# The low part of x: from a GpSimd subtraction to an accumulating DMA and ScalarE, with x and the projection weights split in the opposite sign

## The reference

```
R, K, V = x @ Wr.T, x @ Wk.T, x @ Wv.T
lif:  v = v + (x_t - v) * 0.5;  s = (v >= 1);  v = v * (1 - s)
h = h * 0.9 + k * v;  y = r * h                     # per step, k, v, r are spikes
x1 = layernorm(x + y @ Wo.T) * g1 + b1
s1 = lif_scan(x1 @ W1.T + b1);  ffn = lif_scan(s1 @ W2.T + b2)
a  = layernorm(x1 + ffn) * g2 + b2
x3 = layernorm(x + a)                               # the kernel: mean and variance only
g  = top-2 of softmax(x3 @ Wg + bg), renormalised
out = layernorm(x3 + sum over the 2 chosen experts of g_e * (x3 @ We[e] + be[e]))
```

## Time and profile before

| | us |
|---|---|
| three runs | 1040.43, 1044.15, 1044.51 (median 1044.15) |
| the profiled execution | 1044.85, its span 1043.0 |
| busy: TensorE / VectorE | 965.0 / 965.0 |
| busy: ScalarE / GpSimd | 540.0 / 580.4 |

### The profile page before, as it was taken

The page is one execution under the profiler, slowest core; times in us unless marked ns, Lnnn a source line. Parts: engine busy times, 40 slices in busy tenths (PEclk is TensorE's granted clock), DMA queues, the critical chain, the costliest instruction groups (busy, mean ns, idle before and its releaser), DMA issues.

```text
span 1043.0 us, 22651 instructions
## 1 busy us (share of the span) xinstructions
PE 965.0 (93%) x7552; PEld 935.1 (90%) x7552; DVE 965.0 (93%) x3860; ACT 540.0 (52%) x1256; POOL 580.4 (56%) x720
## 2 busy tenths in 40 slices
PE   5567788999999999999999999999999999899884
PEld 5567777999999999999999999999999999899884
DVE  5888897999999999999999999999999999998765
ACT  4333323456655555555665555555566555455351
POOL 1000122666666676776666666677666666665451
PEclk8878878999999999999999999999999999999998
DMA  4310111344555444544455545454445554446662
GB/s 158 99 52 31 31 41 41 70 91 87 110 102 112 102 104 97 105 101 91 88 108 102 112 102 107 98 102 102 90 87 108 102 112 92 98 95 115 132 126 65
DMA packets 53109, 98.30 MB, mean 94 GB/s; under 512 B 5888, under 2 KB 5888, under 8 KB 52992
## 3 DMA queue, kind: packets, MB, share of 16 engines
q0 software_dynamic: 31392, 57.16, 32.3%
q1 hardware_dynamic: 16992, 31.30, 9.3%
q10 hardware_dynamic: 4608, 8.39, 2.1%
HBM read 31.29 MB, written 8.39 MB: 38 GB/s over the span
## 4 chain that ended last, share of the span: by engine, by line
PE 79%; DVE 14%; ACT 3%; issue 2%; POOL 1%; DMA 0%; POOLq 0%; DVEq 0%; ACTq 0%
PE ps_e L349 30%; PE ps_proj L349 12%; PE ps_proj L404 11%; PE ps_proj L419 9%; PE ps_attn L385 6%; PE ps_proj L425 5%; DVE U L723 3%; DVE V L730 3%; PE ps_zx L393 2%; DVE h L774 1%; PE ps_attn L393 1%; DVE stats L804 1%; POOL s L1161 1%; DVE x_lo L852 1%; ACT x L577 1%
## 5 line engine op out<-in xcount | busy, mean ns | idle before, releaser
L349 PE MATMUL ps_e<-we_hi,x_hi 128*128 128x256 f32 (+1 forms) x1024 | 296.3, 289 | 5.1 <-ACT odd_sum L596 3.2
L349 PE MATMUL ps_e<-we_lo,x_hi 128*128 128x256 f32 (+1 forms) x1024 | 287.6, 281 | 0.0
L349 PE MATMUL ps_e<-we_hi,x_lo 128*128 128x256 f32 (+1 forms) x1024 | 287.5, 281 | 0.0
L730 DVE SCALAR_TENSOR_TENSOR V<-U 128x256 f32<-128x256 f32 (+5 forms) x656 | 249.2, 390 | 0.7
L723 DVE SCALAR_TENSOR_TENSOR U<-V,U 128x256 f32<-128x256 f32 (+5 forms) x656 | 238.0, 373 | 0.9
L559 ACT ACTIVATE U<-ps_proj,cst 128x256 f32<-128x256 f32 x320 | 135.5, 480 | 175.9 <-PE ps_proj L404 98.2
L1147 POOL TENSOR_SCALAR veps<-mv 128x2 f32<-128x2 f32 x128 | 53.9, 421 | 284.1 <-DVE mv L810 284.1
L349 PEld LDWEIGHTS ps_e<-we_hi,x_hi 128*128 128x128 f32 x1024 | 193.5, 189 | 10.6 <-ACT odd_sum L596 8.4
L1161 POOL TENSOR_SCALAR s<-U 128x256 fp32r<-128x256 f32 x208 | 192.5, 951 | 7.7 <-DVE V L730 7.7
L349 PEld LDWEIGHTS ps_e<-we_hi,x_lo 128*128 128x128 f32 x1024 | 193.9, 189 | 0.1
L349 PEld LDWEIGHTS ps_e<-we_lo,x_hi 128*128 128x128 f32 x1024 | 193.1, 189 | 0.0
(11 more groups left out here) (87 smaller groups left out, 2187.7 us busy)
## 6 DMA issues: line engine op xcount, KB each, us to landing
acc<-term POOLq DMA_DIRECT2D x93, 256.0 KB, 3.7
odd_sum<-term POOLq DMA_DIRECT2D x93, 256.0 KB, 3.4
xt<-x_T SPq DMA_DIRECT2D x33, 256.0 KB, 3.0
xa<-x_tok SPq DMA_DIRECT2D x32, 256.0 KB, 3.8
xb<-cst SPq DMA_DIRECT2D x32, 256.0 KB, 2.3
xb<-x_tok POOLq DMA_DIRECT2D x32, 256.0 KB, 6.0
out<-res ACTq DMA_DIRECT2D x32, 256.0 KB, 2.1
term<-w SPq DMA_DIRECT2D x8, 256.0 KB, 5.2
```

The costliest lines, as they stand in the source:

```text
L349: mm = pe.matmul(dst, lhs, rhs, start=(i == 0), stop=(i == n - 1))
L730: v.scalar_tensor_tensor(out=V[:, c0:c1], in0=u, scalar=THRESHOLD, in1=u, op0=ALU.is_lt, op1=ALU.mult).then_inc(done, 1)
```

## The change

- `x_hi` is now the negative of x, rounded; so are `wrkv_hi` and, with them, both low parts. All products keep their sign.
- In all beats but the first, ScalarE writes `x_hi` earlier (`split_x`, right after the projections' results and `gexp`). GpSimd then issues a DMA that adds `x_hi` into the slot of `xt` (`lower_x`), which leaves x minus its high part there. When it has landed (`xt_lowered`), ScalarE writes `x_lo` as the negative of that (`low_x`), at the place where it wrote `x_hi` before.
- GpSimd issues the DMA after `add_odd(7)` and ahead of `reciprocal_std` of the third layer norm. Its subtraction at the end of the beat is gone.
- For the first chunk, VectorE computes `x_lo`, ahead of `wrkv_lo`. `wrkv_lo` becomes a scalar_tensor_tensor.

```diff
--- before.py
+++ after.py
@@ -243,6 +243,7 @@
         wrkv_loaded = [sem(f"wrkv_loaded{f}") for f in range(3)]
         wrkv_hi_ready, wrkv_lo_ready = sem("wrkv_hi_ready"), sem("wrkv_lo_ready")
         x_hi_ready, x_lo_ready = sem("x_hi_ready"), sem("x_lo_ready")
+        xt_lowered = sem("xt_lowered")
         bias_hi_ready, bias_lo_ready = sem("bias_hi_ready"), sem("bias_lo_ready")
         wo_loaded = sem("wo_loaded")
         raw_loaded = [sem(f"raw_loaded{i}") for i in range(RAW_SLOTS)]
@@ -546,6 +547,9 @@
             def copy(out_, in_):
                 return nc.scalar.activation(out_, in_, ACT.Identity)
 
+            def negative(out_, in_):
+                return nc.scalar.activation(out_, in_, ACT.Identity, scale=-1.0)
+
             def to_lif(b, fill, col, tiles, bias):
 
                 bank = b.fills(fill) % 2
@@ -602,7 +606,11 @@
 
                 if b.has(LAG_RKV):
                     act.wait_ge(proj_filled, b.fills(3))
-                copy(x_hi[:], xt[:, b.slot(LAG_X, 2)]).then_inc(x_hi_ready, 1)
+                negative(x_hi[:], xt[:, b.slot(LAG_X, 2)]).then_inc(x_hi_ready, 1)
+
+            def low_x(b):
+                act.wait_ge(xt_lowered, b.value(16, LAG_X + 1, 16))
+                negative(x_lo[:], xt[:, b.slot(LAG_X, 2)]).then_inc(x_lo_ready, 1)
 
             def normalised(ln, dst, src):
 
@@ -635,6 +643,8 @@
 
                     act.wait_ge(gate_steps, b.value(GATE_STEPS, LAG_M, 7))
                     nc.scalar.activation(gexp[:], gdiff[:], ACT.Exp).then_inc(gexp_ready, 1)
+                if b.has(LAG_X) and b.k > LAG_X:
+                    split_x(b)
                 if b.has(LAG_S):
 
                     if b.has(LAG_Z):
@@ -678,12 +688,14 @@
                     if some(b.value(1, LAG_M)):
                         act.wait_ge(bias_done, b.value(1, LAG_M))
                     copy(gate_T[:], ps_attn[0:STACK, :, 0:P]).then_inc(gateT_ready, 1)
-                if b.has(LAG_X):
+                if b.k == LAG_X:
                     split_x(b)
+                elif b.has(LAG_X):
+                    low_x(b)
                 if b.k == LAG_X:
                     for f in range(3):
                         act.wait_ge(wrkv_loaded[f], 16)
-                        copy(wrkv_hi[:, f, :], wrkv_raw[:, f, :]).then_inc(wrkv_hi_ready, 1)
+                        negative(wrkv_hi[:, f, :], wrkv_raw[:, f, :]).then_inc(wrkv_hi_ready, 1)
                 if b.has(LAG_M) and not b.last_m:
                     for e in (5, 6, 7):
                         read_expert(b, e)
@@ -1125,10 +1137,14 @@
             v.memset(V[:], 0.0).then_inc(vec_set, 1)
             v.memset(h[:, STEPS - 1, :], 0.0).then_inc(vec_set, 1)
             v.memset(gate_parts[:].bitcast(F32), 0.0).then_inc(vec_set, 1)
+            dve.wait_ge(x_hi_ready, 1)
+            v.scalar_tensor_tensor(out=x_lo[:], in0=xt[:, 0], scalar=-1.0, in1=x_hi[:].bitcast(F32),
+                                   op0=ALU.mult, op1=ALU.subtract).then_inc(x_lo_ready, 1)
             for f in range(3):
                 dve.wait_ge(wrkv_hi_ready, f + 1)
-                v.tensor_tensor(wrkv_lo[:, f, :], wrkv_raw[:, f, :], wrkv_hi[:, f, :].bitcast(F32),
-                                ALU.subtract).then_inc(wrkv_lo_ready, 1)
+                v.scalar_tensor_tensor(out=wrkv_lo[:, f, :], in0=wrkv_raw[:, f, :], scalar=-1.0,
+                                       in1=wrkv_hi[:, f, :].bitcast(F32),
+                                       op0=ALU.mult, op1=ALU.subtract).then_inc(wrkv_lo_ready, 1)
             dve.wait_ge(vec_set, 3)
             dve.wait_ge(bias_hi_ready, 1)
             rows = slice(ROW_HL, STACK)
@@ -1163,10 +1179,11 @@
                                            THRESHOLD, None, ALU.is_ge)
                 last.then_inc(s1_ready, 2)
 
-            def split_x(b):
+            def lower_x(b):
                 pool.wait_ge(x_hi_ready, b.value(1, LAG_X, 1))
-                g.tensor_tensor(x_lo[:], xt[:, b.slot(LAG_X, 2)], x_hi[:].bitcast(F32),
-                                ALU.subtract).then_inc(x_lo_ready, 1)
+                g.dma_start(xt[:, b.slot(LAG_X, 2)].rearrange("p k n -> p (k n)"),
+                            x_hi[:].bitcast(F32).rearrange("p k n -> p (k n)"),
+                            accum_op=ALU.add).then_inc(xt_lowered, 16)
 
             def add_even(b, lag, e):
 
@@ -1215,6 +1232,8 @@
                     reciprocal_std(b, 1, ln2_steps, LN2_STEPS, LAG_Z, 4)
                 if sums:
                     add_odd(b, LAG_F, 7)
+                if b.has(LAG_X) and b.k > LAG_X:
+                    lower_x(b)
                 if has_z:
                     reciprocal_std(b, 2, ln3_steps, LN3_STEPS, LAG_Z, 4)
                 if has_m and not b.last_m:
@@ -1223,8 +1242,6 @@
                     reciprocal_std(b, 3, fin_steps, FIN_STEPS, LAG_F, 6)
                 if has_m and not b.last_m:
                     add_odd(b, LAG_M, 3)
-                if b.has(LAG_X):
-                    split_x(b)
 
             g.memset(neg_half[:], -0.5).then_inc(pool_set, 1)
             pool.wait_ge(pool_set, 1)
```

## The result

| | us |
|---|---|
| before, median of 4 runs | 1042.84 (1040.43 to 1044.51) |
| changed, median of 4 runs | 1029.61 (1029.46 to 1030.79) |
| ratio | 0.9882, 95% interval 0.9869 to 0.9895 |
| profiled executions | 1044.85 before, 1029.46 changed |

A forecast was written before the change was run, and what follows sets the result against it. TensorE's matmuls were taken to bound steady beats, VectorE's LIF, h and y chain beats 0 to 5. Terms +0.3, -4.6 and -1.0 gave -5.3 us from the profiled 1044.85: 1039.5 us, range 1034.5 to 1044.5.

The forecast's parts named there:

- The block's size: VectorE standing still beside GpSimd's subtraction: about 1.1 us in a steady beat, 0.87 to 1.04 in beats 1 to 5.
- steady beats give nothing: In the 24 or so steady beats TensorE's matmuls set the length, so removing VectorE's block gains 0.
- Beat 31: First beat without a new projection behind it: the block ends in the y TensorE waits for; removing it gives -1.0 us.
- The DMA: GpSimd's DMA adding x_hi into xt: 3.6 us from issue to landing, in steady beats 7.7 us before ScalarE needs it.
- B: Steady beats get shorter too, at most 9 us; half of that gives 1034.8 us; chance 0.12.
- D: The DMA's issue blocks VectorE as the subtraction did, a block only 0.3 us shorter in seven places: 1044.2 us; chance 0.08.
- E: The DMA lands late in steady beats, over 11.3 us, and ScalarE, carrying TensorE's input, waits: 1064.9 us; chance 0.06.
- Five blocks, 4.6 us: Beats 1 to 5, where the pipeline fills: five blocks on VectorE's chain go, -4.6 us in total.
- The first `w_lo`: VectorE's operation in beat -1, behind the DMA and ScalarE's low_x: starts at 18.7 us, before 17.34, so +1.4.
- The sum: Whole kernel: +0.3 for beats -1 and 0, -4.6 for beats 1 to 5, -1.0 for beat 31: -5.3 us, 1039.5.
- rival C: The fill eats its gain: DMA lands after 6.0 us (+2.4), TensorE's clock falls once more (+2.5): 1044.4 us; chance 0.24.
- the waits for y stay near 22 us: First 290 us: TensorE's waits for VectorE's y stay near 22 us in 6 times, since both sides move.

The follow-up runs named there:

- e2: Kernel before, with GpSimd writing zeros into x_lo instead of subtracting up to beat 5 only, the true subtraction from beat 6 on: 1032.59 us, ratio 0.9903.
- e1: Kernel before, with GpSimd writing zeros into x_lo instead of subtracting in all beats, order and waits unchanged: 1031.90 us, ratio 0.9905.
- e4: Kernel before, with matmuls of no use ahead of TensorE's wait for y in the beats before 7: 1035.86 us, ratio 0.9945.
- e6: Kernel before, with 32 more accumulating DMAs of 256 KB on GpSimd's queue, one per beat, result not used: 1038.67 us, ratio 0.9962.
- e8: Kernel before, with 8 more unused accumulating DMAs of 256 KB on GpSimd's queue, in beats 7 to 14: 1043.31 us, a single run.
- e3: Changed kernel, with an unused GpSimd subtraction of the old size put back at the end of each beat from -1 on: 1040.38 us, ratio 0.9983.
- after_again: The changed kernel, unaltered, measured again later on another chip: 1030.51 us, ratio 0.9902.
- e9: Changed kernel, with matmuls of no use ahead of the wait for y before beat 7 and the unused GpSimd subtraction put back: 1034.99 us, ratio 0.9943.
- e10: Changed kernel, with VectorE writing the second chunk's low part and matmuls of no use ahead of all TensorE's waits in beats 1 to 6: 1021.06 us, ratio 0.9808.

## Why the prediction was wrong

**What held.** The block's size and that it vanishes. That steady beats give nothing: 694.81 against 695.07 us. Beat 31: -0.95 (predicted -1.0), of which e2 against e1 shows the block as the cause. The first matmul at 5.59 us (predicted 5.5 to 5.6). The DMA: 4.2 us to land (3.6; by its own sign, 3.4 to 3.9, a little late), and hidden in steady beats with 8.3 us to spare (7.7). Rivals B, D and E did not occur. "Five blocks, 4.6 us", measured with TensorE's clock alike on both sides: 4.2 and 5.2.

**What came out by luck.** The first `w_lo` at 18.1 (18.7): `x_hi` started at 12.12 where 13.25 was forecast, 1.1 us sooner, and from its end to `x_lo` there were 4.2 us where the sum had 3.6, 0.6 more; the two partly cancel. And the level of the forecast had an error of its own: the 5.3 us were taken from the profiled execution of 1044.85, 2.0 above the median of before, so of the 9.9 us between 1039.5 and 1029.61 some 2 are the base and 7.9 the gain.

**The step that failed first: the clock, priced on one side only.** "The sum" took each microsecond of VectorE's as one of the total, and let TensorE's clock in only as rival C, as a loss. But the fill of before was paying for its slow stretches: the earlier trace rows had 0.79 there, and keeping TensorE busy was worth 7 us in before by itself (e4). Two of the groups that run at half speed before run at full speed in the changed kernel's first profile. Between first and sixth mark the profiles of before and its likes (e6, e8) have 135.6 to 138.3 us and those of the changed kernel 126.1 and 128.8, some 9 us less, where the blocks are worth 4.2 to 5.2: about 4 to 5 us by the clock, as the remainder. Taken from single pairs of profiles the remainder is anything from 1.6 to 8.0 us, and of the 9.9 us of whole time on the second chip only about 2 are left for it, after blocks of 4.6 and 0.95 and a DRAIN of 2.5: its sign is shown, its size only roughly. What raised it is not settled: it rises when the blocks go and x_lo stays early (e1, e2: 126.8 and 129.3 us), and it is at 0.86 also when the blocks stay and x_lo is late (e3: 132.2). Over the first 190 us the granted clock is 0.82 in before, 0.85 in e6 and 0.83 in e8, 0.86 in e3, 0.87 in e1 and e2, 0.86 and 0.87 in the changed kernel. In the same way "the waits for y stay near 22 us" was wrong: they are 16.3 in 6 times (17.1 in after_again; 18.7 and 20.5 in e1 and e2, 20.4 in e3).

```profile
PE ps_attn L386 <- DVE y L809: 16.3, 6, 7.1
```

Rival C's mechanism, a slow stretch of TensorE that costs time in the fill, is real (e4), and it works with either sign: in the profiles it about doubled what this change's blocks give in the fill. Which beats it hits wasn't to be read from the trace of before, and e3 and e1, with different starts, have it at different places. That it could fall on the side of a gain was.

**The second: the last instruction was never priced.** The sum had no term for the end of the program. GpSimd's DRAIN was 7.25 us in the trace of before and ended 0.2 us before the span did; the change, by adding 32 DMAs to GpSimd's queue, shortened it by 2.49 (e6 has the same with DMAs of no use). The size I could not have forecast from one trace, but it shows that the end hangs on this instruction.

**The third, small:** two slow stretches in the last 90 us of before, none in the changed kernel's profile; worth about 2 us (between the mark at 929.30 and the last statistics at 1034.96 there are 105.7 us, against 103.6 in the changed kernel). The other profiles have one or two, so this part is a matter of the single execution, and about the 2.2 us by which the difference of the profiled executions (15.4) exceeds that of the medians (13.2).

The account of the profiled executions: blocks 4.2 to 5.2 in the fill and 0.95 in beat 31, clock in the fill 4.3 to 5.3 as what is left of 9.5, DRAIN 2.5, clock at the end 2.0, steady beats and start 0.4: 15.3. The blocks and the DRAIN are measured by runs of their own; the clock's share is a remainder, good to about 3 us. Open: which part of the change raised TensorE's clock in the fill, what in the number or bytes of the DMAs sets the DRAIN's length, and why the block costs 1.5 us in the steady beats of e9.

## What to carry to other kernels

When the bound of a stretch is a chain on one engine and TensorE idles in it at a lowered clock, price a shortened chain twice, once for itself and once for TensorE's clock, with both signs; a few matmuls of no use ahead of the wait show in one run how much the clock is worth. Compare marks within the program as well as whole times, and take two profiles of each kernel: here two of one kernel differed by up to 2.7 us in the fill. Read the last instruction of every engine, above all GpSimd's, before forecasting a change to the number of its DMAs. The GpSimd subtraction of 1.29 us, which reads SBUF, cost VectorE 0.9 to 1.1 us in nearly every place where it fell beside a two-input instruction; where VectorE bounds the stretch, move such an operation or turn it into a DMA.

## What the runs showed of the hardware

- GpSimd's DRAIN at the end of the program: 7.25 us with 218 DMAs issued on its queue, 4.92 with 226, 4.76 with 249 and 250, the same to 0.01 us in all profiles with the same count.
- GpSimd's memset of 128x512 (0.53 us) doesn't stretch VectorE's two-input instruction beside it (U x2 at 0.45, e1), its subtraction of the same size does (four h in 1.86 instead of 0.87, e9). The Trainium skill, page "SBUF — State Buffer", section "Who interferes with whom", says that only a GpSimd instruction that reads SBUF contends with such an instruction; the runs agree.
- GpSimd issues the DMA in 0.86 to 1.23 us (median 1.20) and it lands 3.3 to 4.9 us after its issue (median 4.2) with VectorE busy for 27.5 of 29 us beside it; no starvation of the queue was seen.
- Eight matmuls 128x256 in fp32 take 3.78 us at the lower level of the clock and 1.99 at the upper. After 4.3 us of idle TensorE they ran at the lower one, after 0.62 and 2.45 us at the upper; but the wait alone doesn't decide it, since in e10 a group behind 2.35 us took 3.09, in e3 one behind 3.12 us took 1.99, and in the changed kernel those behind 0.92 and 0.46 us (at 125.88 and 153.99) took 3.78.
